# A decoder layer on one core: the end of each sequence and the start of the next moved below the main steps, all decays in two PSUM banks

## What is computed

```python
# for each of the 4 sequences
a  = retention(x)                # 16 heads of 16, decay mask gamma**(n-m), group norm per head,
x1 = layernorm(x + (silu(x@wg+bg) * a) @ wo + bo)            # gate, output projection, norm
u  = silu(causal_conv4(ctx @ in_proj))                       # 256 channels
dt, Bm, Cm = x_proj(u)                                       # 8, 16, 16 rows
delta = softplus(dt_proj(dt) + dtb)
for t in range(256):                                         # selective scan, 16 states a channel
    state = state * exp(delta[t] * A) + delta[t] * u[t] * Bm[t]
    y[t] = (state * Cm[t]).sum(states)
x2 = layernorm(x1 + (y + D*u) * silu(x1))
top2 of softmax(x2 @ Wg.T) over 8 experts, weights rw
for k in 0, 1:                                               # the expert is a rank-32 addition
    x1_ = x2@W1.T + (mask_k * (x2@A1)) @ B1;  x3_ = x2@W3.T + (mask_k * (x2@A3)) @ B3
    h = silu(x1_) * x3_                                      # 896 wide
    out += rw_k * (h@W2.T + (mask_k * (h@A2)) @ B2)
y = layernorm(x2 + out)
```

## Time and profile before

| | us |
|---|---|
| median of 3 runs | 470.35 |
| the profiled execution, its own time | 471.16 |
| its span, first to last instruction | 469.4 |
| TensorE matmuls busy, in the span | 388.2 (83%) |
| VectorE busy | 327.9 (70%) |
| GpSimd busy | 234.1 (50%) |
| ScalarE busy | 186.9 (40%) |
| mean granted TensorE clock | 0.929 of full |

### The profile page before, as it was taken

The page is one execution under the profiler, slowest core; times in us unless marked ns, Lnnn a source line. Parts: engine busy times, 40 slices in busy tenths (PEclk is TensorE's granted clock), DMA queues, the critical chain, the costliest instruction groups (busy, mean ns, idle before and its releaser), DMA issues. The chain is left out here.

```text
span 469.4 us, 7131 instructions
## 1 busy us (share of the span) xinstructions
PE 388.2 (83%) x2552; PEld 330.3 (70%) x2552; DVE 327.9 (70%) x631; ACT 186.9 (40%) x417; POOL 234.1 (50%) x219
## 2 busy tenths in 40 slices
PE   3766989898763968899797889979678998889993
PEld 2544767776542656899676789966568997779983
DVE  5436485676758379998588999858899995652224
ACT  3673447375134285252238425223852520231100
POOL 6014454364532058978305897740589784042121
PEclk9957899999786879999998899999899999999999
DMA  7541270100010311212012121201222220000000
GB/s 219 218 184 40 80 246 6 43 1 1 24 34 0 83 34 46 89 46 67 13 40 76 68 88 48 68 1 43 73 68 76 61 68 0 1 24 0 2 0 22
DMA packets 12338, 27.02 MB, mean 58 GB/s; under 512 B 1800, under 2 KB 3088, under 8 KB 12048
## 3 DMA queue, kind: packets, MB, share of 16 engines
q1 hardware_dynamic: 11872, 25.79, 16.9%
q10 hardware_dynamic: 432, 0.79, 0.4%
HBM read 25.39 MB, written 1.18 MB: 57 GB/s over the span
## 5 line engine op out<-in xcount | busy, mean ns | idle before, releaser
L976 PE MATMUL xf<-am,wsplit 128*128 128x256 f32 x672 | 97.1, 294 | 9.6 <-DVE am L1678 4.9
L976 PEld LDWEIGHTS xf<-am,wsplit 128*128 128x128 f32 x672 | 87.7, 194 | 13.2 <-issue 6.1
L541 POOL TENSOR_TENSOR ring<-cv,brow 128x512 f32<-128x512 f32 x48 | 78.3, 1649 | 6.5 <-PE acc L976 4.0
L976 PE MATMUL a2p<-work,wff_sb 128*128 128x256 f32 x224 | 58.7, 385 | 4.0 <-POOL work L653 4.0
L945 ACT ACTIVATE fth<-xf 128x256 f32<-128x256 f32 x56 | 21.3, 380 | 100.4 <-PE xf L976 100.4
L976 PE MATMUL xf<-x2s,wsplit 128*128 128x256 f32 x336 | 50.3, 301 | 5.9 <-ACT work L925 5.6
L1764 DVE SCALAR_TENSOR_TENSOR fth<-fth,xf 128x256 f32<-128x256 f32 x56 | 23.1, 413 | 44.2 <-ACT fth L945 44.1
L695 ACT ACTIVATE decay<-dt_w,nega 128x255 f32<-128x255 f32 x80 | 36.1, 500 | 42.8 <-DVE ring L1569 30.8
L653 POOL TENSOR_TENSOR work<-work,ratioT 128x256 f32<-128x256 f32 x28 | 23.8, 851 | 55.0 <-DVE work L1775 49.6
L976 PEld LDWEIGHTS xf<-x2s,wsplit 128*128 128x128 f32 x336 | 44.5, 198 | 8.3 <-ACT work L925 6.4
L1516 DVE TENSOR_TENSOR ring<-ring,crow 128x512 f32<-128x512 f32 x36 | 43.3, 1203 | 3.7
(11 more groups left out here) (244 smaller groups left out, 728.7 us busy)
## 6 DMA issues: line engine op xcount, KB each, us to landing
brow<-bc_dram SPq DMA_DIRECT2D x24, 256.0 KB, 3.5
crow<-bc_dram SPq DMA_DIRECT2D x24, 256.0 KB, 3.3
work<-in_wsp SPq DMA_DIRECT2D x3, 896.0 KB, 8.9
wff_sb<-in_wff SPq DMA_DIRECT2D x2, 896.0 KB, 7.6
am<-bc_dram SPq DMA_DIRECT2D x1, 1536.0 KB, 7.6
wattn_sb<-in_wattn SPq DMA_DIRECT2D x1, 1280.0 KB, 5.6
xT_sb<-in_xT SPq DMA_DIRECT2D x4, 256.0 KB, 2.7
xn_sb<-in_x SPq DMA_DIRECT2D x4, 256.0 KB, 2.6
```

The lines of the kernel that those rows point to most:

```text
L541: pool.tensor_tensor(ring[:, i % RING], du[:, j].unsqueeze(1).broadcast_to([P, UN, S]), brow[:, c % 2], ALU.mult).then_inc(sem["drive_read ...
L976: return pe.matmul(o, l, r, skip_group_check=True, **kw)
```

## The change

1. **Units move forward.** In `first` 21 slots stand in place of 16; the units are done in slots 0 to 10, two in every odd one (`FIRST_UNITS`). In a stage the last unit is scanned in step 9 and added in step 10 (`SCANS`, `SUMS`).
2. **`seam` and `later` are gone.** Their work for the finished sequence (cross, norm, flip, logits, routing, spreading, masked inputs) and the prelude of the next (context, convolution, low rank, step size, du, first two drives and decays) is written into steps 7 to 13 and behind them, and in `first` into slots 8 to 17. The routing of sequence 0 so runs beside the attention of sequence 3.
3. **Decays.** All units of a stage have their decays in PSUM, the even ones in `gens[1]`, the odd ones in `ret`. The scan runs in place there, and VectorE multiplies all 16 by C, from PSUM into the ring. GpSimd's four are dropped. Decays of unit i wait for the product with C of unit i - 2; those of unit 0 for the fourth masked input of the sequence before (which is read from the same bank).
4. **Downs.** As `ret` holds decays, a stage's first `down` is in step 10: steps 10 to 13 hold six, the seventh stands behind them. The last stage has them spread from step 4 on.
5. **Banks and tiles.** x2's transpose, logits, A1, A3, route rows and masks go through `GEN`, no longer through `xf`. Masks, x2's split, delta and other tiles are doubled or moved; small sets are shared; `r1` is kept in `xn_sb`, so the next load of x is issued from ScalarE's queue after the norm of the sequence before it (SP did it before).
6. **Attention.** The output projection of sequence s - 2 moves from the second to the first slot of a sequence, its residual on VectorE to the second.

The diff, cut to its core:

```diff
+SLOTS = 21
+FIRST_UNITS = {0: (0,), 1: (1, 2), 2: (3,), 3: (4, 5), 4: (6,), 5: (7, 8), 6: (9,), 7: (10, 11), 8: (12,), 9: (13, 14), 10: (15,)}
...
-SCANS = [[0], [1], [2], [3, 4], [5], [6], [7], [8, 9], [10], [11, 12], [13, 14], [15], [], []]
-SUMS = [[], [0], [1], [2], [3], [4, 5], [6], [7], [8], [9, 10], [11], [12], [13, 14], [15]]
-DOWNS = {5: (0,), 6: (1,), 9: (2,), 10: (3,), 12: (4,)}
+SCANS = [[0], [1, 2], [3], [4, 5], [6, 7], [8], [9, 10], [11, 12], [13, 14], [15], [], [], [], []]
+SUMS = [[], [0], [1], [2, 3], [4, 5], [6], [7, 8], [9, 10], [11, 12], [13, 14], [15], [], [], []]
+DOWNS = {10: (0, 1), 11: (2,), 12: (3, 4), 13: (5,)}
+DOWNS_LAST = {4: (0,), 5: (1,), 8: (2,), 9: (3,), 12: (4,), 13: (5,)}
...
         def decay_of(b, i):
-            return v3(gens[1], S) if b > 0 and i in BANKED else decay[:, SLOT.get(i, i % 2) if b > 0 else i % 2]
+            if b == 0:
+                return decay[:, i % 2]
+            return v3(gens[1], S) if i % 2 == 0 else ret[:]
...
@@ GpSimd, first and stage
+                    if i == 16:
+                        inputs(nb)
+                        drive_unit(nb, 0)
+                        drive_unit(nb, 1)
+                        bias(B - 1)
+                        second_masks(b)
...
+                if nb is not None:
+                    inputs(nb)
+                    drive_unit(nb, 0)
+                    drive_unit(nb, 1)
+                if b is not None:
+                    second_masks(b)
@@ ScalarE
+                if b == 0:
+                    need(act, "state_ready", b, max(i - 1, 0))
+                elif i >= 2:
+                    need(act, "out_dve", b - 1, i - 1)
+                elif i == 0 and b == 1:
+                    need(act, *emptied(previous(1, GEN.index(("Z", 1)))))
+                elif i == 0:
+                    need(act, "am_ready", b - 1, 4)
...
+                if b > 0:
                     act.activation(to[:, :, 0:1], mhalf[:].unsqueeze(2), ACT.Copy, scale=0.0)
...
@@ ScalarE, stage, behind step 13
+                if nb is not None:
+                    softplus_log(nb)
                 if b is not None:
-                    seam(b, nb)
+                    routed(b)
+                    spread(b)
+                    am_high(b, (0, 1))
+                if nb is not None:
+                    decays(nb, 0)
+                if b is not None:
+                    am_high(b, (2, 3))
+                if nb is not None:
+                    start_y(nb)
+                    decays(nb, 1)
+                if b is not None:
+                    ratios(b)
@@ TensorE, stage
+                    if nb is not None:
+                        if n == 7:
+                            context(nb)
+                        if n == 11:
+                            low_rank(nb)
+                    if b is not None and n == 11:
+                        flip_x2(b)
+                    if nb is not None and n == 12:
+                        step_size(nb)
+                    if b is not None and n == 12:
+                        logits(b)
...
+                    if b is not None and n == 13:
+                        expert_inputs(b, "A1", A1)
+                        expert_inputs(b, "A3", A3)
+                if b is not None:
+                    route_rows(b)
                 shrink(fb, len(MAIN) - 1)
                 if b is not None:
-                    seam(b, fb, nb)
...
+                    base(b, 1)
+                    spread_rows(b, "MK", 0)
+                    spread_rows(b, "MD", 1)
+                down(fb, FM - 1)
+                if b is not None:
+                    base(b, 0)
+                end_sum(fb)
+                if b is not None:
+                    spread_rows(b, "RW", 2)
@@ VectorE, scan and times_c
-                unit = flat(ring[:, i % RING])
-                dve.tensor_tensor_scan(unit, flat(decay_of(b, i)), unit, 0.0,
-                                       ALU.mult, ALU.add).then_inc(sem["state_ready"], 1)
+                bank_ = flat(decay_of(b, i))
+                dve.tensor_tensor_scan(bank_, bank_, flat(ring[:, i % RING]), 0.0, ALU.mult, ALU.add
+                                       ).then_inc(sem["state_ready"], 1)
...
-                unit = ring[:, i % RING]
-                dve.tensor_tensor(unit, unit, crow[:, c % 2], ALU.mult).then_inc(sem["out_dve"], 1)
+                dve.tensor_tensor(ring[:, i % RING], decay_of(b, i), crow[:, c % 2], ALU.mult).then_inc(sem["out_dve"], 1)
@@ VectorE, stage
+                    if n == 9 and nb is not None:
+                        conv(nb)
+                    if n == 10 and b is not None:
+                        crossed(b)
+                        norm_stats(b, r2, st, mv, ve, "r2_ready", 3)
+                    if n == 10 and nb is not None:
+                        conv_gate(nb)
+                    if n == 12 and b is not None:
+                        second_part(b)
+                        route(b, 0)
                     if n == 13:
                         second_input(fb, 0)
                 if b is not None:
+                    route(b, 1)
+                if nb is not None:
+                    step_small(nb)
+                    step_sum(nb)
+                if b is not None:
+                    masked_inputs(b, (0, 1))
                 second_input(fb, 1)
                 need(dve, "a2_ready", fb, 2)
                 dve.tensor_tensor(a2m[:, 0], a2m[:, 0], a2m[:, 1], ALU.add).then_inc(sem["a2_ready"], 1)
...
+                    input_lows(b)
+                    masked_inputs(b, (2, 3))
```

758 lines of the change are left out of this document (382 added, 376 removed).

## The result

The change made the kernel slower: 480.15 us median of 4 runs (480.07 to 481.88), against 471.25 (470.17 to 472.19) for the kernel before on the same chip, a ratio of 1.0198 with a 95% interval of 1.0161 to 1.0236. Forecast were 464.0, in a range of 449 to 477: both the number and the side were wrong. The profiled execution has a span of 478.5 us against 469.4.

A forecast was written before the change was run, and what follows sets the result against it. TensorE and VectorE, nearly equally busy, take turns waiting; the new scan stretch is VectorE's, the tail TensorE's. Handover at 246.3, plus stages of 82.2 and 78.2, then 55.4 plus 0.8: span 462.9, about 464 us, range 449 to 477.

The forecast's parts named there:

- The new scan stretch: Handover to end of step 9: 16 units at 1.93 us on VectorE, with waits, 49.8 us.
- The new tail: Start of step 10 to handover, mostly TensorE's queue: 32.4 us, making the steady stage 82.2 against 82.6.
- The first sequence: Slot 14 at 133.5, handover at 152.5 against 173.3; double slots counted at nothing, priced at 0 to 8 us.
- From slot 14 to the handover: TensorE's and ScalarE's work from slot 14 at 133.5 us to the first handover at 152.5.
- But a chain stands behind it: After the first handover: serial links over four engines put step 0's first product at about 173, against 177.41.
- The sum: Whole program: handovers at 246.3 and 406.7, last stage 55.4 plus 0.8, span 462.9, time about 464.
- (2): Rival: double slots lose their cover and the handover chain grows by 5: 469 us, chance 0.16.
- (3): Rival: TensorE's clock falls in the scan stretch; at 60% half-clock work 4.6 us more three times: 478 us, chance 0.12.
- (4): Rival: PSUM does not shield VectorE's product with C, 27 us on the bound engine: 491 us, chance 0.06.
- (1): Rival: downs and shrinks slip into TensorE's idle time, stages 76 each, 14 us less: 450 us, chance 0.18.

The follow-up runs named there:

- e2: Changed kernel with router logits ahead of the next step size on TensorE, and router exponential ahead of the softplus on ScalarE: 472.49 us, ratio 1.0007.
- e3: Changed kernel with both scans of a first-sequence double slot ahead of that slot's decayed score products on VectorE: 474.46 us, ratio 1.0058.
- e8: Changed kernel with 8 unread matmuls filling TensorE's wait for x2 in slot 12, ahead of the flip: 479.39 us, ratio 1.0166.
- e12: e10 with slot 12's score products ahead of x2's normalisation shift on VectorE, and x2 flipped in slot 13 behind the scores: 453.40 us, ratio 0.9612.
- e1: Changed kernel with sequence 3's gate ahead of bias, mask sum and low parts on GpSimd at the first handover: 477.03 us, ratio 1.0104.
- e13: e7 with ScalarE's copy of the ratio rows, which empties bank 0, ahead of the next sequence's first decays: 461.54 us, ratio 0.9784.
- e10: e7 with sequence 3's output projection, residual, statistics and normalisation moved from the first handover into steps 1 to 3 of the next stage: 454.96 us, ratio 0.9650.
- e11: Changed kernel with 17 unread matmuls ahead of sequence 3's output projection on TensorE: 480.61 us, ratio 1.0182.
- p1: Kernel before with only the PSUM decays, scans and products, scans ended at step 9, downs at steps 10 to 12, no overlap: 471.52 us, ratio 0.9996.
- e7: Changed kernel with e1, e2 and e3 together, plus sequence 3's linear normalisation part ahead of the next first decays on ScalarE: 462.62 us, ratio 0.9806.
- e6: Changed kernel with 24 unread matmuls ahead of sequence 3's output projection on TensorE: 482.61 us, ratio 1.0220.

## Why the prediction was wrong, point by point

Two steps of the prediction failed: the tail's queue, taken at 32.4 us and measured at 37.0, and the first sequence up to slot 14, where a term was put at nothing and measured at 6.3 of the 10.1 us that were missing.

**The new scan stretch: right.** "I take 0.61, by the scan that lost its disturbance the same way": the product took 0.692 busy, without spread, and the next instruction started 0.61 behind it (301.01 to 301.62). The stretch from handover to the end of step 9, set at 49.8, was 48.4 in the second stage (261.0 to 309.4). The wait for the table load was there, 1.28 us with nothing behind it: it starts at 261.24 and the exponential at 262.53, so the trace's price holds. The Trainium skill's 2.66 (ScalarE: Activation LUTs, What ACT_TABLE_LOAD costs) isn't seen here, nor the 4 us that the range held for it.

**The new tail: the failing step of the stages.** "Behind it everything is in one queue", and "flip, step size, logits, route rows and two spreads, estimated 4.1 from matmul counts": I counted the work in the queue and not the bank that two neighbours share. The step size stands ahead of the logits in bank 0, so TensorE waits until ScalarE has emptied it, and then works at half clock. The handover came at 37.0 after the start of step 10, not 32.4; e2 takes 4.7 off, which leaves 32.3. So the sum was right for the kernel that e2 is, its parts less so: x2 is flipped 6.1 us into step 10, for 5.4. The 4.6 is most of the 5.1 of stage one (78.4 for 73.3; the other 0.5 lies in its scan stretch) and, less the 1.4 that the scan stretch came in under, the 3.2 of stage two (85.4 for 82.2). The third has no next sequence and came at 76.8 for 78.2.

**The first sequence: "I count nothing for that, the cover being the waits these slots had, and price it at 0 to 8 us".** The value taken was wrong, the bound was right. e3 puts the order of the scans at 6.3 us. The cover I named did not exist for the work that mattered: the waits of those slots were VectorE's, and what the second scan held up were TensorE's drives. The rest up to the 10.1 us that slot 14 was late (143.6 for 133.5), 3.8 us, I put down to slots 12 and 13 of the changed kernel:

```profile
129.52 1.12 PE L1431 MATMUL xf<-ident,x 128*128 128x128 f32 x4 [2.53 <-ACT x L953]
...
134.66 2.07 PE L1051 MATMUL gen<-vpad,ratioT 128*128 128x128 f32 x8 [2.01 <-DVE sc L1614]
136.53 1.72 PE L1051 MATMUL gen<-wroute_sb,kT 128*128 128x8 f32 x8
138.86 1.90 PE L1051 MATMUL gen<-u,wssm_sb 128*40 128x256 f32 x4 [0.62 <-DVE u L1543]
```

TensorE waits 2.53 us for x2, 2.01 for the score products and 0.62 for u, and from 130 to 142 the granted clock was 0.50. I had put a length on the work there and none on the waits. e8 and e12 show that no one of these waits decides it; what the two together are worth was not separated, so this part of the cause stays open.

**From slot 14 to the handover: right**, 18.6 us for 19.0. **"But a chain stands behind it": right in size.** 20.5 us were worked out from the handover to the first product, and 20.4 measured, in the queues named. The closeness is in part luck: the links written out add up to 18.3 to 19.8, and the part from the residual to the first product took 5.8 us (176.72 to 182.56) for 4.8. Of the 20.4, e1 takes 3.3 off by GpSimd's order, e13 another 3.1 by ScalarE's, and e10 shows 9 more that needed no place there. One link was missing: the projection also waits for bank 0, which ScalarE's last copy empties. It was hidden as long as the gate was later.

**The sum.** It was 15.6 us too low in span: 9.6 before the first product of step 0, 5.1 and 3.2 in stages one and two, less 1.4 and 0.9 in the last two. Against the kernel before, the first product is 5.2 us later, stage two 2.8 and stage three 1.2 longer: that is the 9.1 of the two spans.

**The rivals.** (2) came by half: the double slots lost their cover, 6.3 of the 0 to 8 us, while the handover chain did not grow (20.4 for 20.5). At 469 it fell short, since the tail's wait was not in it. (3) placed the half clock in the scan stretch and needed 45% of the work there at it. In stage two's scan stretch the granted clock was 0.96: half clock from 265.6 to 269.0, behind a wait of 2.78 us that ended at 265.33, and 1.00 from there to the end of step 9. The longer stretch, 323.6 to 330.4, fell behind the wait at a shared bank, where I had not looked. The Trainium skill's rule (TensorE: Matmul & The Clock Gate, What's actually happening), that the throttled state is the default and activity releases it, agrees with e11, where the projection took 1.97 us instead of 3.75 once matmuls filled the wait. (4), that PSUM does not shield the product, is out by 0.692. (1) was argued away because "nothing slips"; the tail of 32.3 in e2 agrees with that. No rival named a bank shared between two engines' work: the only ones that ended well on the slow side needed the clock or PSUM to fail, and so "slower" got 0.18.

## What to carry to other kernels

When work of two sequences is laid side by side, list for every shared PSUM bank who fills it, who empties it, and where the emptier stands in its own queue. Two neighbours in one queue that share a bank are a wait of the emptying engine's length, and here it cost 1.4 to 3.0 us in TensorE's clock on top of the 1.66 of waiting (C of e2 against e8 and against the changed kernel). Freeing a busy engine moved nothing by itself here (p1), as another engine's work only shifted from one part of the stage to the other. And a step that is moved forward brings its successors' chain into the open: ask for each link whether the next stage needs it before its first step, and put what it doesn't need behind that step.

## What the runs showed of the hardware

- TensorE's granted clock fell to half (1.2 GHz) at waits as short as 1.66 us, and stayed there for a while when work was back. These are 8 us from the start of the logits in the changed kernel, in e8 with the same wait, and in e2 without it; the granted clock is the third column from the end:

```profile
238.10:246.10 8.00, 8.00 (x30) 6.92 (x31) 0.87 (x5) 0.43 (x1) 0.00 (x0) 0.57 0.09 34
```
```profile
239.50:247.50 8.00, 8.00 (x39) 7.08 (x40) 1.50 (x7) 1.56 (x4) 0.00 (x0) 0.79 0.06 22
```
```profile
237.80:245.80 8.00, 8.00 (x45) 6.81 (x46) 4.04 (x14) 1.78 (x6) 1.35 (x2) 1.00 0.33 106
```

  In the changed kernel the logits, the downs and a shrink ran at half clock until about 245.0, in e8 only what stood between about 240.3 and 243.8. Nor does the length of a wait decide it alone: in the kernel before, three waits of 1.82 us for x2 left TensorE at its upper level (2.4 GHz):

```profile
234.54 0.63 PE L1329 MATMUL xf<-ident,x 128*128 128x128 f32 x4 [1.82 <-ACT x L900]
```

- Stretches of one and the same program differ by up to 1.8 us from one kernel to another, with the granted clock: C is 73.7 in e7 at 0.98 and 75.5 in e13 at 0.95, D is 82.3 in e10 at 0.96 and 80.7 in e12 at 0.98. A difference below 2 us in a stretch is read beside its granted clock.
- With one operand in PSUM VectorE's product isn't disturbed: 691 to 694 ns in 48 cases. GpSimd's drive product beside it is disturbed less: a median of 1.29 us for 1.72, the longest 1.80 for 2.21.
- A record of an fp32 matmul is half of one here: 24 instructions show as x48. One of 128x256 took 0.46 us at full clock (8 in 3.70 us in e8, at a granted clock of 1.00) and 0.498 on average in e6, where the first 3 us were at half clock.
